# A Perceiver block on one core: order of the value splits, of batch 0's setup, and of the expert weights' loads and rooms

## The reference

```
x = x + cross(norm(x), ctx)      # scores = (x w1' + b1) ctx' / 16; softmax; weights @ ctx; [x, that] w2' + b2
x = x + local(norm(x))           # 16 heads, windows of 64 over all 1024 rows
x = x + experts(norm(x))         # top 2 of 8 experts: (silu(x wg') * (x wu')) wd', weighted
```

## Time and profile before

| | us |
|---|---|
| runs | 637.23, 634.75, 634.33 (median 634.75) |
| profiled execution | 640.98 |
| its span, first to last instruction | 639.2 |
| busy in the span | PE 581.6, DVE 405.7, ACT 331.8, POOL 259.6 |
| mean granted TensorE clock | 0.98 of full speed |

### The profile page before, as it was taken

The page is one execution under the profiler, slowest core; times in us unless marked ns, Lnnn a source line. Parts: engine busy times, 40 slices in busy tenths (PEclk is TensorE's granted clock), DMA queues, the critical chain, the costliest instruction groups (busy, mean ns, idle before and its releaser), DMA issues.

```text
span 639.2 us, 9964 instructions
## 1 busy us (share of the span) xinstructions
PE 581.6 (91%) x3765; PEld 493.5 (77%) x3765; DVE 405.7 (63%) x703; ACT 331.8 (52%) x564; POOL 259.6 (41%) x250
## 2 busy tenths in 40 slices
PE   7887989888988898988999999999999999999795
PEld 5666888788777887976776677888888878888684
DVE  5634367445844485537898978867676766767551
ACT  4335633654346443552867673656556464656350
POOL 4583418441755166433444532233424142423122
PEclk9897999999989999999999989999999999999899
DMA  8991039002910020000000594899999989999442
GB/s 298 422 413 68 2 145 368 13 1 83 393 52 1 1 67 2 1 1 1 1 2 2 193 398 156 322 347 337 337 335 331 349 305 347 317 352 329 142 149 82
DMA packets 22223, 119.27 MB, mean 187 GB/s; under 512 B 2640, under 2 KB 8912, under 8 KB 14096
## 3 DMA queue, kind: packets, MB, share of 16 engines
q1 hardware_dynamic: 17808, 112.48, 46.5%
q0 software_dynamic: 4368, 6.16, 4.6%
HBM read 113.52 MB, written 6.42 MB: 188 GB/s over the span
## 4 chain that ended last, share of the span: by engine, by line
PE 67%; DVE 11%; DMA 7%; ACT 6%; issue 4%; POOL 4%; POOLq 0%; SPq 0%; ACTq 0%; DVEq 0%
PE psum L1634 15%; PE psum L1413 13%; PE psum L1651 11%; PE psum L1367 10%; PE psum L1271 9%; DMA region_w<-normed_rows,tokens 5%; ACT wide_high L668 2%; POOL wide_low L557 2%; ACT region_s L707 2%; PE psum L1329 2%; DVE wide_low L974 2%; DVE turned_low L1027 2%; DVE head_max L943 2%; DVE region_a L948 1%; PE psum L1304 1%
## 5 line engine op out<-in xcount | busy, mean ns | idle before, releaser
L668 ACT ACTIVATE wide_high<-region_a 128x1024 fp32r<-128x1024 f32 (+1 forms) x108 | 107.4, 994 | 105.1 <-PE psum L1634 101.2
L1101 DVE TENSOR_TENSOR wide_low<-region_a,wide_high 128x1024 fp32r<-128x1024 f32 x92 | 112.3, 1223 | 59.0 <-ACT wide_high L668 59.0
L1413 PE MATMUL psum<-turned_high,wide_low 128*128 128x256 f32 x256 | 80.4, 314 | 28.3 <-DVE turned_low L1027 27.8
L1651 PE MATMUL psum<-region_a,region_w 128*128 128x256 f32 x368 | 83.3, 379 | 0.0
L1634 PE MATMUL psum<-wide_low,turned_high 128*128 128x512 f32 x184 | 78.8, 428 | 0.3 <-DVE turned_high L1203 0.2
L1651 PEld LDWEIGHTS psum<-region_a,region_w 128*128 128x128 f32 x368 | 69.6, 190 | 10.0
L1413 PEld LDWEIGHTS psum<-turned_high,wide_low 128*128 128x128 f32 x256 | 50.0, 195 | 32.4 <-issue 32.3
L668 ACT ACTIVATE turned_high<-psum 128x512 fp32r<-128x512 f32 x64 | 38.2, 597 | 70.3 <-PE psum L1413 64.1
L1027 DVE TENSOR_TENSOR turned_low<-psum,turned_high 128x512 fp32r<-128x512 f32 x64 | 42.8, 686 | 49.7 <-ACT turned_high L668 49.7
L1413 PE MATMUL psum<-turned_low,wide_high 128*128 128x256 f32 x256 | 73.5, 287 | 0.0
L1413 PE MATMUL psum<-turned_high,wide_high 128*128 128x256 f32 x256 | 73.5, 287 | 0.0
(11 more groups left out here) (220 smaller groups left out, 1198.7 us busy)
## 6 DMA issues: line engine op xcount, KB each, us to landing
region_a<-up_weights_dram SPq DMA_DIRECT2D x23, 2048.0 KB, 9.7
region_a<-down_weights_dram SPq DMA_DIRECT2D x23, 1024.0 KB
region_w<-ctx_cols_dram SPq DMA_DIRECT2D x32, 512.0 KB, 9.0
region_a<-ctx_dram SPq DMA_DIRECT2D x16, 1024.0 KB, 11.8
third_weights<-third_weights_dram SPq DMA_DIRECT2D x1, 1035.0 KB, 25.4
residual<-x_dram SPq DMA_DIRECT2D x4, 256.0 KB, 7.2
sums_by_token<-residual SPq DMA_DIRECT2D x2, 512.0 KB, 9.3
normed_rows<-region_s SPq DMA_DIRECT2D x4, 256.0 KB, 6.5
```

The source lines that it names most:

```text
L668: return nc.scalar.activation(dst, src, ACT.Copy)
L1101: nc.vector.tensor_tensor(w_lo[:, k % RING], group_of(k), w_hi[:, k % RING].bitcast(F32), ALU.subtract).then_inc(low_ready, 1)
L1413: last = nc.tensor.matmul(bank[6 + c][:, 0:NTOK], v[:, value_slot(b, g), k, c * P:(c + 1) * P], p[:, g % 2, k, :], start=g == 0 and k == 0 ...
L1651: last = nc.tensor.matmul(to[:, 0:D], hidT[n][:, ic * P:(ic + 1) * P], rows, start=ic == 0, stop=ic == IC - 1)
```

## The change

- **Values.** `value_low(3)` before the first `probs_low` goes, and after an odd group g DVE subtracts the values of group g + 2, where it was g + 4.
- **Batch 0.** Statistics of batches 1 to 3 go from ahead of the chunks to behind chunks 0, 1, 2; their normalising from behind chunks 0, 1, 2 to behind 2, 3, 4 (into other places of the score region). PE turns all three behind chunk 5, in banks of their own, and ACT copies them behind its last chunk. `ON_POOL[0]` goes from 2, 4, 6, 7 to 1, 3, 5, 7. `add_b2` goes from behind POOL's chunks into its value groups, and the wait for b2 goes with it.
- **Up weights** lie in DRAM as two halves of 8 KB rows, where they were one of 16 KB rows; one transfer still loads both.
- **Down weights** get a third room, where the normalised rows lay, and are loaded one tile further ahead, at the same point of SP's order.

```diff
-SETUP_AT = {0: 1, 2: 2, 4: 3}
+DOWNS = 3
+SETUP_AT, SETUP_BANK = CHUNKS - 3, [6, 7, 0, 1]
+STATS_AT, NORM_AT, ADD_AT = [0, 1, 2], [2, 3, 4], [2, 6, 8, 10]
-ON_POOL = [[2, 4, 6, 7], [2, 4, 6], [2, 4, 6], [2, 4, 6]]
+ON_POOL = [[1, 3, 5, 7], [2, 4, 6], [2, 4, 6], [2, 4, 6]]
...
-        w_down = [region_a[:, (4 + n) * MAT:(5 + n) * MAT] for n in range(2)]
+        w_down = [region_a[:, 4 * MAT:5 * MAT], region_a[:, 5 * MAT:6 * MAT], region_s[:, 0:MAT]]
...
-                sp.dma_start(w_up[n], rows.rearrange("a p n -> p (a n)")).then_inc(up_loaded[n], 16)
+                sp.dma_start(w_up[n].rearrange("p (m n) -> p m n", m=2), rows.rearrange("a m p n -> p (a m) n")).then_inc(up_loaded[n], 16)
...
+                if j == DOWNS - 1:
+                    sp.wait_ge(rows_stored, 16 * DUOS)
+                if j >= DOWNS:
+                    sp.wait_ge(y_done, j - DOWNS + 1)
...
             for j in range(2, SLOT_TILES):
                 if j + 1 < SLOT_TILES:
                     load_up(j + 1)
-                if j > 2:
-                    load_down(j - 1)
-            load_down(SLOT_TILES - 1)
+                load_down(j)
...
-                    if b == 0:
-                        add_b2(ON_POOL[0].index(ch))
...
+                    if b == 0 and g in ADD_AT:
+                        add_b2(ADD_AT.index(g))
...
-                        if b == 0 and ch - 1 in SETUP_AT:
-                            setup_copy(SETUP_AT[ch - 1])
+                    if b == 0:
+                        for s in range(1, BATCH):
+                            setup_copy(s)
...
-                        if b == 0 and ch < BATCH - 1:
-                            normalise(0, ch + 1, xn[ch + 1])
+                        if b == 0 and ch in STATS_AT:
+                            s = STATS_AT.index(ch) + 1
+                            dve.wait_ge(x_loaded[s], 16)
+                            statistics(range(s * TPB, (s + 1) * TPB))
+                        if b == 0 and ch in NORM_AT:
+                            s = NORM_AT.index(ch) + 1
+                            normalise(0, s, xn[s])
...
                     value_low(1)
-                    value_low(3)
...
-                        if g % 2 == 1 and g + 4 < PAIRS:
-                            value_low(g + 4)
+                        if g % 2 == 1 and g + 2 < PAIRS:
+                            value_low(g + 2)
...
-                        if b == 0 and ch in SETUP_AT:
-                            setup_turn(SETUP_AT[ch])
+                        if b == 0 and ch == SETUP_AT:
+                            for s in range(1, BATCH):
+                                setup_turn(s)
```

More of the change, by code:

```diff
@@ L108, in perceiver @@
         raw = [region_w[:, n * DC * BANK:(n + 1) * DC * BANK].rearrange("p (c n) -> p c n", c=DC) for n in range(RAW)]
-        xn = [scores[0][:, (BATCH + s) * BANK:(BATCH + s) * BANK + TPB * D].rearrange("p (t d) -> p t d", t=TPB) for s in range(BATCH)]
+        xn = [scores[s % 2][:, (CHUNKS - 2 + s // 2) * BANK:(CHUNKS - 1 + s // 2) * BANK].rearrange("p (t d) -> p t d", t=TPB) for s in range(BATCH)]
         qT_f, k_side_f, v_wide_f, sl0, sl1, sl2, sl3 = cut(region_a, [DC * TOK, SIDES * DC * TOK, BATCH * KEPT] + [HPC * P] * 4)
@@ L268, in perceiver @@
         up_loaded = [sem(f"up_loaded{n}") for n in range(UPS)]
-        down_loaded = [sem(f"down_loaded{n}") for n in range(2)]
+        down_loaded = [sem(f"down_loaded{n}") for n in range(DOWNS)]
         xg_loaded = [sem(f"xg_loaded{n}") for n in range(AHEAD)]
@@ L392, in expert_of @@
                 sp.wait_ge(owner_ready, 1)
-                return rows[bass.ds(sp.value_load(owner[0:1, j - E:j - E + 1], min_val=0, max_val=E - 1), 1), :, :]
+                return rows[bass.ds(sp.value_load(owner[0:1, j - E:j - E + 1], min_val=0, max_val=E - 1), 1)]
             def load_up(j):
@@ L542, in rows_biased @@
                                         ALU.add).then_inc(biased, 1)
-            pool.wait_ge(b2_loaded, 16)
             def add_b2(b):
                 part = xr[:, b * TPB:(b + 1) * TPB, :]
+                pool.wait_ge(b2_loaded, 16)
                 pool.wait_ge(xn_ready, (b + 1) * TPB)
@@ L593, in _ @@
                     rows_biased(BATCH - 1)
-            pool.indirect_dma_start(out=xg[AHEAD - 1], out_offset=None, in_=up_weights.rearrange("e p (a n) -> (e p a) n", n=D),
+            pool.indirect_dma_start(out=xg[AHEAD - 1], out_offset=None, in_=up_weights.rearrange("e m p (a n) -> (e m p a) n", n=D),
                                     in_offset=bass.IndirectOffsetOnAxis(ap=spare_i[:, 0:1], axis=0)).then_inc(spare_gathered, 16)
@@ L671, in setup_copy @@
                 act.wait_ge(setup_turned, b + 1)
-                copy(xnT[:, :, b * NTOK:(b + 1) * NTOK], bank[6 + b % 2].rearrange("p (c n) -> p c n", c=DC)).then_inc(setup_out, 1)
+                copy(xnT[:, :, b * NTOK:(b + 1) * NTOK], bank[SETUP_BANK[b]].rearrange("p (c n) -> p c n", c=DC)).then_inc(setup_out, 1)
             def queries_high_part(b):
@@ L718, in _ @@
                             queries_high_part(0)
-                        if b == 0 and ch == 1:
-                            for s in range(1, BATCH):
-                                deviation(0, s)
+                        if b == 0 and ch - SPLIT in STATS_AT:
+                            deviation(0, STATS_AT.index(ch - SPLIT) + 1)
+                        if b == 0 and ch == CHUNKS - 2:
                             act.wait_ge(consts, N_CONST)
                             nc.scalar.activation(act_pause[:, 1:2], zeros[:, 0:1], ACT.Exp)
-                        if b == 0 and ch - 1 in SETUP_AT:
-                            setup_copy(SETUP_AT[ch - 1])
+                    if b == 0:
+                        for s in range(1, BATCH):
+                            setup_copy(s)
                     if b > 0:
@@ L1004, in _ @@
                         queries_low(0)
-                        for s in range(1, BATCH):
-                            dve.wait_ge(x_loaded[s], 16)
-                            statistics(range(s * TPB, (s + 1) * TPB))
                     for ch in range(CHUNKS):
@@ L1287, in setup_turn @@
                     for t in range(TPB):
-                        last = turn(bank[6 + b % 2][:, (c * TPB + t) * P:(c * TPB + t + 1) * P], xn[b][:, t, c * P:(c + 1) * P])
+                        last = turn(bank[SETUP_BANK[b]][:, (c * TPB + t) * P:(c * TPB + t + 1) * P], xn[b][:, t, c * P:(c + 1) * P])
                 last.then_inc(setup_turned, 1)
@@ L1643, in tile_down @@
             def tile_down(j, n, part=range(IC), to=bank[6]):
-                pe.wait_ge(down_loaded[n], 16 * (j // 2 + 1))
+                pe.wait_ge(down_loaded[j % DOWNS], 16 * (j // DOWNS + 1))
                 if 0 < j < SLOT_TILES - 1:
@@ L1649, in tile_down @@
                         pe.wait_ge(hidT_ready, j * 2 + ic // TPG + 1)
-                    rows = w_down[n][:, ic * D:(ic + 1) * D]
+                    rows = w_down[j % DOWNS][:, ic * D:(ic + 1) * D]
                     last = nc.tensor.matmul(to[:, 0:D], hidT[n][:, ic * P:(ic + 1) * P], rows,
```

8 lines of the change are left out of this document (2 added, 6 removed).

## The result

| | before | after |
|---|---|---|
| runs, median | 634.85 us (634.33 to 637.23) | 601.54 us (601.21 to 609.83) |
| profiled execution, its span | 640.98, 639.2 | 601.86, 600.1 |
| PE busy, share of the span | 91% | 95% |

The ratio is 0.95, with an interval of 0.9415 to 0.9584. A second set of runs gave 601.24 (600.55 to 602.51), 0.9443 (0.9388 to 0.9499). Forecast: 600.0, in 591 to 613.

The account below looks back on a forecast made before the run. PE was taken as the bound, with its waits and the slow clock after them. Terms 7.9 + 16.4 + 4.0 + 3 + 7 = 38.3 us gave 596.5, or 603.5 without the experts' loss; middle 600, range 591 to 613.

Parts of the forecast that it names:

- starts, other waits and clock of the weighings: Weighings: values two groups ahead save 7.9 us at four starts, 16.4 in other waits, 4.0 of slow clock.
- batch 0's chunks: Batch 0: 8.0 us to be had, less 5.2 of new waits from DVE and POOL splits colliding; 3 taken.
- experts: Expert tiles: 8 KB up-weight rows make scatters land sooner, so late gathers end; 7 of 7.9 us taken.
- the 0.8 kept back for other waits: Weighings: of 17.2 us in 13 waits, 0.5 left for group 3 of batch 1 and 0.3 elsewhere.
- The rival of another wait taking over: Weighings: half of 16.4 us and a third of the start lost, about 611 us; chance 0.13.
- the clock's 1.3: Batch 0's chunks: 1.3 us taken of at most 2.1 us lost to the slow clock.
- The rival without collisions: Batch 0: DVE and POOL splits do not collide, 4.6 us more gained, 595 us; chance 0.15.
- the step that was to give them: Experts: scatter falls from 9.1 to 6 or 7 us, so POOL's cycle no longer reaches 10.04 us per tile.
- Moved waits and third room: POOL's additions of b2, ACT's copies and the third room for down weights: no effect on time.
- the middle of 603.5 and 596.5: Whole kernel's median: 603.5 us if timed runs lacked the experts' loss, 596.5 if they had it; 600 taken.
- The branch without the experts' loss: Whole kernel: timed runs lacked the late gathers, so they gain 31.3 us from 634.75, giving 603.5.
- Slower by expert loads: Experts: 8 KB rows cost transfer rate and PE waits for up weights; 650 us at 280 GB/s; chance 0.03.

Follow-up runs that it names:

- ACT earlier: Kernel before, with ACT making the values' high part five groups ahead and DVE's order unchanged: 610.13 us, ratio 0.9564.
- early splits: Changed kernel, batch 0's DVE splits of chunks 2, 4, 6 one chunk earlier, statistics and ACT's deviations moved to match: 595.03 us, 0.9343; once more 595.51, 0.9349.

## Why the prediction was right, step by step

The profiled executions differ by 39.1 us; the sum said 38.3. Its terms, by stage (a weighing runs from the projection behind a batch's chunks to the end of its last group, both by the chain in order of time):

| term | forecast | measured |
|---|---|---|
| starts, other waits and clock of the weighings | 7.9 + 16.4 + 4.0 = 28.3 | 31.5 (9.63, 6.63, 8.63, 6.60 by batch) |
| batch 0's chunks | 3 | 1.4 (44.08 to 42.67) |
| experts | 7 | 6.1 (209.00 to 202.88) |
| sum | 38.3 | 39.0 |

- **Value order: right, under-sized by 3.2.** The waits fell by 27.8 - 3.4 = 24.4, where 7.9 + 16.4 = 24.3 was said: starts wait 1.07 and not 0.9, and of the 0.8 kept back for other waits 0.2 was needed. What the sum lacked is that a wait costs PE 0.23 us more than the list says, as the groups of the experiment with ACT earlier show. With 13 waits fewer that is 3.0. The waits fell by 6.4, 5.9, 6.4 and 5.7 us in batches 0 to 3. In batches 1 and 3, which lost nothing to the clock, these and the surcharge for 3 and 4 waits give 6.6 and 6.6, and 6.63 and 6.60 were measured. In batches 0 and 2 some 4.1 us are left for the clock, where 4.0 was said. The prediction tied a fall of the clock to the length of the wait before it. That isn't the whole rule: batch 1's start waited 2.89 and the clock between 117 and 128 us was 1.00. The rival of another wait taking over falls: no wait of the weighing is above 1.07.
- **Batch 0: right mechanism, gain half of the forecast.** The waits were forecast at 5.2 and are 5.4, so the 1.5 us by which they were to shrink came as 1.4. Their parts differ: 1.93 and 2.55 for 2.2 and 3.0, and a third of 0.89 ahead of chunk 6 that the prediction did not have, because it let only splits meet splits. A normalising is blocked as well (2.92 for 0.74). What is missing from the 3 is the clock's 1.3: the clock stayed at 0.94 in this execution. In the repetition, with the same code, the same waits and a clock of 1.00, the chunks gain 2.3 (44.08 to 41.82); first the change, then its repetition:

```profile
42.67 1.73 PE psum L1306 x8
```

```profile
41.82 1.73 PE psum L1306 x8
```

  The Trainium skill ("SBUF — State Buffer", section "SBUF: two separate sides") calls the port pair an exclusive lock; the rows of 3.09 against 1.19, and of 2.89 for POOL where DVE came first, agree. The rival without collisions, 595, is about what the early splits gave: 595.0.
- **8 KB rows: worth something, but the size came by luck.** The 6.1 us are near the 7 forecast, but the step that was to give them did not happen: POOL still waits 56.8 us in 9 waits for its own transfer, for 61.1 in 9. What was large was the loss of the one profiled execution before. (It was 7.6 and not 7.9 over the 11 tiles, with 10.07 us per tile for 10.04. The fall of the clock behind the longest wait, which rows 12 do not show, is there: 0.72 between 599 and 605 us.) Over all profiled executions the 20 tiles took 209.00, 202.0, 201.46, 203.6, 203.2, 207.95 and 205.08 us with 16 KB rows (mean excess over 201.47: 3.1), and 202.88 once and 201.47 or 201.48 five times with 8 KB (mean excess 0.2). POOL waited for its own transfer 9, 1, 0, 13, 4, 9 and 7 times with 16 KB, and 9, 1, 1, 0, 0 and 0 times with 8 KB. So late gathers are rarer with shorter rows; by medians or ratios that is worth 3.9 us alone, 2.5 in the change and 4.3 with early splits.
- **How shorter rows do it: not shown.** That each small packet waits half as long isn't borne out: the median landing of the scatter was 5.9 to 9.1 us with 16 KB, 6.6 to 7.9 with 8 KB and 7.5 with 4 KB, and that of the gather 7.0 to 8.0, 7.4 to 7.7 and 7.4. The scatter's landing is no mark of late gathers either: it was 7.8 where POOL waited nine times, 7.2 with nine waits in the kernel with ACT earlier, and 7.9 with none in the early splits. What starts a run of late scatters stays open. Nor is it borne out that nothing changes, which the prediction drew from the Trainium skill ("DMA: Bandwidth & Descriptors", section "Queues, rings and completion order"). That page puts many descriptors into a packet; if their number were fixed, halving each would halve the packet, so what it states doesn't decide the matter.
- **Moved waits and third room: right**, no wait shows there, and the room alone has a ratio of 0.9999.
- **From profile to median.** I took the middle of 603.5 and 596.5. The branch without the experts' loss was the nearer: the execution of before had 7.5 us of it over the 20 tiles, and 640.98 - 7.5 = 633.5 is 1.4 below the median. The median thus gained 33.3, about the 31.5 + 1.4 of the other stages. With the terms as measured, that branch gives 634.75 - 32.9 = 601.9. So 600 lies so near to 601.5 in part by luck: by the forecast's own terms this branch gives 603.5, the middle took 3.5 off for a loss that the timed runs mostly had not, and the weighings gave 3.2 more than their terms while batch 0 gave 1.6 less.
- **Slower by expert loads**: no wait for up weights, at 8 or at 4 KB.

The four parts alone sum to 30.8 + 3.9 + 0.7 + 0.1 = 35.5 us by their ratios; by its ratio the whole gave 31.7 in the first set and 35.5 in the second. They add up within intervals of 3 to 6 us each, which would not show a small interaction between the parts.

## What to carry to other kernels

When an engine waits in order for something that it needs only later, move the instruction behind the work that is ready: here two changed lines gave about 31 of 35 us, while the other three parts together were worth about 5. Before moving work between DVE and POOL, lay out by the microsecond which of their SBUF operations meet, all of them and not the largest alone; a microsecond in the arrival decides who is late. A wait costs more than the list says; compare the length of the same groups with and without it. A profiled execution may hold a loss that the median run has not: compare it with the spread of the runs before adding its stages to the sum.

## What was not expected of the hardware

- A DVE operation with one SBUF tensor input is also held up by POOL's subtraction of two: 0.74 us alone, 2.31 to 2.92 beside it. Who comes first pays little: DVE's split at 15.24 took 1.22, POOL's behind it 2.89. The trace of the kernel before had this already. The normalising at 22.58 takes 1.41 for 0.74 and ends just behind POOL's addition:

```profile
22.58 1.41 DVE L903 TENSOR_SCALAR region_s<-residual,ln_mean_var,ln_rstd 128x256 f32<-128x256 f32 x2
```

```profile
22.24 1.28 POOL L548 TENSOR_TENSOR residual<-residual,b_rows 128x512 f32<-128x512 f32 x1
```

- The row length of the weight loads seems to bear on how steadily another queue's small transfers land. With 16 KB rows the 20 tiles varied by 7.5 us over seven executions, with 8 KB by 1.4 over six, at the same bytes; the rate was 336 and 339 GB/s in the two stretches shown. The executions are few, and of several kernels.
- The same kernel had a clock of 0.96 and of 1.00 over its first 46 us in two executions.
